# Layer-norm statistics of a convolution and mixture-of-experts kernel: from two matmul groups on TensorE to block transposes and free-axis sums on VectorE

## What is computed

```python
x = x + _L0_conv_ref(_ln_c(x), ...)
t = _to_tokens(x)
t = t + _L0_ffn_ref(_ln_t(t), ...)
...
def _ln_t(v, eps=1e-05):
    m = jnp.mean(v, axis=-1, keepdims=True)
    s = jnp.var(v, axis=-1, keepdims=True)
    return (v - m) / jnp.sqrt(s + eps)
```

## Time and profile before

| | us |
|---|---|
| median of 3 runs | 1285.11 (1285.0 to 1286.29) |
| profiled execution, its own time | 1287.97 |
| its span | 1286.2 |
| TensorE busy | 1251.1 (97%) |
| VectorE busy | 849.1 (66%) |
| ScalarE busy | 820.8 (64%) |
| GpSimd busy | 666.8 (52%) |

### The profile page before, as it was taken

One profiled execution on the slowest core, in us unless ns is written; L12 is line 12 of the kernel. 1 busy time (PEld: TensorE's weight loads), 2 busy tenths in 40 slices (PEclk: granted clock), 3 DMA queues, 4 the chain that ended last, 5 costly groups with the idle time before them and its releaser, 6 DMA issues. The chain is left out here.

```text
span 1286.2 us, 36567 instructions
## 1 busy us (share of the span) xinstructions
PE 1251.1 (97%) x14628; PEld 622.3 (48%) x14628; DVE 849.1 (66%) x1495; ACT 820.8 (64%) x1046; POOL 666.8 (52%) x607
## 2 busy tenths in 40 slices
PE   6999989999999999999999999999999999999897
PEld 4789744444444444444444444444444444444553
DVE  5444656676677677677677677677677777666554
ACT  5677756666666666666666666666667666666443
POOL 0151514645665655665655665655665655665532
PEclk9999999999999999999999999999999999999899
DMA  9897502332333332343342343332343333333211
GB/s 215 198 200 198 109 16 59 87 81 58 79 87 79 86 82 56 79 93 72 86 87 56 74 94 72 87 86 65 68 89 78 81 87 75 65 84 75 57 30 30
DMA packets 262694, 111.28 MB, mean 87 GB/s; under 512 B 243336, under 2 KB 247008, under 8 KB 262624
## 3 DMA queue, kind: packets, MB, share of 16 engines
q1 hardware_dynamic: 261360, 108.87, 37.8%
q0 software_dynamic: 1264, 1.61, 0.6%
HBM read 84.25 MB, written 26.17 MB: 86 GB/s over the span
## 5 line engine op out<-in xcount | busy, mean ns | idle before, releaser
L1031 DVE SCALAR_TENSOR_TENSOR v<-ps,negb,wb 128x448 f32<-128x448 f32 x896 | 573.2, 679 | 309.9 <-PE ps L642 307.3
L843 ACT ACTIVATE h<-ps,bias 128x896 f32<-128x896 f32 x448 | 450.2, 1005 | 292.5 <-PE ps L620 289.5
L660 PE MATMUL ps<-v,wo 64*64 64x448 f32 x3584 | 449.3, 541 | 7.1 <-issue 6.8
L620 PE MATMUL ps<-xn,w 64*64 64x448 f32 x3584 | 444.7, 542 | 2.2 <-issue 2.1
L642 PE MATMUL ps<-h,w 64*64 64x448 f32 x3584 | 444.4, 538 | 1.7 <-issue 1.3
L495 POOL TENSOR_TENSOR sums<-sums 128x448 f32<-128x448 f32 x112 | 127.9, 1142 | 306.2 <-ACT sums L849 306.2
L642 PEld LDWEIGHTS ps<-h,w 64*64 64x64 f32 x3584 | 170.7, 133 | 174.8 <-issue 156.1
L660 PEld LDWEIGHTS ps<-v,wo 64*64 64x64 f32 x3584 | 158.3, 133 | 173.5 <-issue 159.1
L620 PEld LDWEIGHTS ps<-xn,w 64*64 64x64 f32 x3584 | 141.7, 132 | 188.9 <-issue 187.4
L489 POOL TENSOR_TENSOR o<-xin,gconst 128x448 f32<-128x448 f32 x112 | 126.2, 1139 | 162.4 <-DMA out<-o 97.1
L499 POOL TENSOR_TENSOR o<-o,sums 128x448 f32<-128x448 f32 x112 | 133.6, 1193 | 8.8
(11 more groups left out here) (167 smaller groups left out, 552.1 us busy)
## 6 DMA issues: line engine op xcount, KB each, us to landing
xa<-in_x SPq DMA_DIRECT2D x128, 196.0 KB, 5.0
xin<-in_x SPq DMA_DIRECT2D x224, 112.0 KB, 2.8
out<-o SPq DMA_DIRECT2D x224, 112.0 KB, 2.5
spread<-rs_rows SPq DMA_DIRECT2D x108, 224.0 KB, 4.2
wb<-gate_rows SPq DMA_DIRECT2D x54, 112.0 KB, 2.8
rs_rows<-rs SPq DMA_DIRECT2D x54, 7.0 KB
gate_rows<-wT SPq DMA_DIRECT2D x54, 1.8 KB
rows<-in_L_ffn_g POOLq DMA_DIRECT2D x2, 256.0 KB, 4.7
```

Source lines behind the costliest of these rows:

```text
L620: last = mm(ps[64 * two:64 * two + 64, L1_BANKS + ab, 0:NG], w1[half, P * q + C * two:P * q + C * two + C], xn[half, s, g, :], start=True, ...
L660: last = mm(ps[64 * par:64 * par + 64, ACC_BANKS + low, 0:NG], wo[rows_, 2 * Q + d, :], v[rows_, u % 2, par, d, :], start=(Q == 0 and d == ...
L843: A(h[:, u % 2, i], ps[:, L1_BANKS:L1_BANKS + 2, 0:NG], ACT.Relu, bias=bias[:, 0, q:q + 1]).then_inc(h_done[i], 1)
L1031: last = V.scalar_tensor_tensor(out=v[:, u % 2, ab, d, :].rearrange("p (b w) -> p b w", w=W), in0=ps[:, L2_BANKS[ab] + d, 0:NG].rearrange( ...
```

## The change

From chunk 1 on the sums over the channels are no longer matmuls over the data. (Chunk 0, prepared ahead of the loop, keeps the old way.)

- Behind each x1, VectorE transposes the group in blocks of 32x32 into t (a block has 32 channels and 32 tokens), so that a partition holds a token of a block and the 32 channels lie along the free axis (`turned_done`). A reduce per group then adds them: 128x448 to 128x14, in token_sums (place **means**).
- ScalarE squares the transposed t instead of xin. GpSimd (`halve_powers`, behind `add_upper(k, 1)` and `add_upper(k, 2)`) adds one half of the 32 squares to the other, 128x448 out of two groups' 128x896, and VectorE reduces the rest (place **fold**), to 128x28 for two groups.
- TensorE adds only the two blocks of 32 channels of each row: two 64x64 matmuls by 112 columns at place 52, with same_token. They wait for `summed_done` and `powers_summed`.
- Variance, root and inverse are 128x56 instead of 128x448. VectorE turns the result (128x64) and SyncE writes it to rs_rows as 64 pieces of 128 bytes per half instead of 4 rows; the broadcast back has the same size.
- The places move: x1 from 16, 21, 36, 39 to 12, 18, 24, 30, that is ahead of the first taking of u2, u3, u4 and u5. inv from 58 and 60 to 60 alone. SyncE's order of loads and stores is as before, and so are t's places on ScalarE.

```diff
         LOOPED = (RP - 1 - 2) // 2 * 2
-        LOOP_SLOT = 128
+        LOOP_SLOT = 156
...
         STEADY = Schedule(
-            t=(9, 15, 21, 27), x1=(16, 21, 36, 39), power=(33, 43), sums=52,
-            var=54, root=56, inv=(58, 60), logits=85, gate=86, turn=89, wb=94)
+            t=(9, 15, 21, 27), x1=(12, 18, 24, 30), means=(36, 36, 42, 42), power=(33, 43), fold=(42, 48), sums=52,
+            var=54, root=56, inv=(60, 60), logits=85, gate=86, turn=89, wb=94)
...
+                def halve_powers(q, p):
+
+                    pool.wait_ge(squares_done, STEPS * q + p + 1)
+                    parts = spread[:, 2 * p:2 * p + 2].rearrange("p g (k two c) -> p two (g k) c", two=2, c=TOKENS // 2)
+                    nc.gpsimd.tensor_tensor(parts[:, 0], parts[:, 0], parts[:, 1], ALU.add).then_inc(powers_halved, 1)
...
                     add_upper(k, 1)
+                    if left > 1:
+                        halve_powers(k + 2, 0)
                     add_upper(k, 2)
+                    if left > 1:
+                        halve_powers(k + 2, 1)
...
                             pe.wait_ge(v_done[0], UNITS * (q - 1) + 2)
+                            pe.wait_ge(summed_done, G * (q - 1) + G)
+                            pe.sem_inc(sums_free, 1)
+                            pe.wait_ge(powers_summed, STEPS * (q - 1) + STEPS)
+                            pe.sem_inc(powers_free, 1)
+                            for hi in range(2):
+                                rows_ = slice(64 * hi, 64 * hi + 64)
+                                last = mm(ps[rows_, Y, 0:2 * G * BLOCKS], same_token[rows_].rearrange("p a c -> p (a c)"),
+                                          token_sums[rows_].rearrange("p a g k -> p (a g k)"), start=True, stop=True)
+                            last.then_inc(power_done, 1)
+                    if h == at.sums and at is AHEAD:
                         pe.wait_ge(x1_done, G * q + G + G)
...
                     for p in places_at(at.power, h):
-                        act.wait_ge(x1_done, G * q + 2 * p + 2 + G)
+                        act.wait_ge(turned_done, G * (q - 1) + 2 * p + 2)
                         act.wait_ge(u_done[p], q + 1)
...
+                        A(spread[:, 2 * p:2 * p + 2], t[:, 2 * p:2 * p + 2], ACT.Square, bias=-1.0).then_inc(squares_done, 1)
...
                                                op0=ALU.min, op1=ALU.add).then_inc(x1_done, 1)
+                        if at is STEADY:
+                            dve.wait_ge(x1_done, G * q + g + 1 + G)
+                            V.transpose(t[:, g], xg.rearrange("p b w -> p (b w)")).then_inc(turned_done, 1)
+                    for g in places_at(at.means, h):
+                        dve.wait_ge(turned_done, G * (q - 1) + g + 1)
+                        V.tensor_reduce(token_sums[:, 0, g, :], t[:, g].rearrange("p (k c) -> p k c", c=TOKENS), AX.X, ALU.add).then_inc(summed_done, 1)
+                    for p in places_at(at.fold, h):
+                        dve.wait_ge(powers_halved, STEPS * (q - 1) + p + 1)
+                        halved = spread[:, 2 * p:2 * p + 2].rearrange("p g (k two c) -> p two (g k) c", two=2, c=TOKENS // 2)[:, 0]
+                        V.tensor_reduce(token_sums[:, 1, 2 * p:2 * p + 2, :].rearrange("p g k -> p (g k)"), halved, AX.X, ALU.add).then_inc(powers_summed, 1)
...
+                            final.then_inc(turn_ready, 1)
+                            dve.wait_ge(turn_ready, q)
+                            V.transpose(rs_turned[:], token_rs[:]).then_inc(rs_done, 1)
```

More of the change, by code:

```diff
@@ L33 @@
 QUADS = E // 4
+TOKENS = 32
+BLOCKS = NG // TOKENS
 UNITS = G * QUADS
@@ L41, with __init__ @@
 class Schedule:
-    def __init__(self, t, x1, power, sums, var, root, inv, logits, gate, turn, wb):
-        self.t, self.x1, self.power, self.sums = t, x1, power, sums
+    def __init__(self, t, x1, means, power, fold, sums, var, root, inv, logits, gate, turn, wb):
+        self.t, self.x1, self.means, self.power, self.fold, self.sums = t, x1, means, power, fold, sums
         self.var, self.root, self.inv = var, root, inv
@@ L165, in metaformer_kernel @@
         squares_done = sem("squares_done")
+        turned_done = sem("turned_done")
+        summed_done = sem("summed_done")
+        powers_halved = sem("powers_halved")
+        powers_summed = sem("powers_summed")
+        powers_free = sem("powers_free")
+        turn_ready = sem("turn_ready")
+        zero_pad = sem("zero_pad")
         means_done = sem("means_done")
@@ L512, in chunk @@
                     add_upper(k, 1)
+                    if left > 1:
+                        halve_powers(k + 2, 0)
                     add_upper(k, 2)
+                    if left > 1:
+                        halve_powers(k + 2, 1)
                     if not left:
                         add_upper(k, G - 1)
+                for p in range(STEPS):
+                    halve_powers(1, p)
                 body_of_chunks(chunk)
@@ L867, in prep @@
                         A(t[:, g].rearrange("p (b w) -> p b w", w=W), yq, ACT.Relu, bias=OFFSET1, scale=SCALE).then_inc(t_done, 1)
-                    if h == at.sums:
+                    if h == at.sums and at is STEADY:
+                        act.wait_ge(power_done, q + 1)
+                        A(token_mean2[:], ps[:, Y, 0:G * BLOCKS], ACT.Square, bias=-1.0).then_inc(mean2_done, 1)
+                    if h == at.sums and at is AHEAD:
                         act.wait_ge(means_done, q + 1)
@@ L966, in _ @@
                 V.tensor_tensor(pick[:], row_of[0], row_of[1], ALU.add)
+                V.memset(token_rs[:], 0.0)
+                step(V.tensor_reduce(same_token[:, 0, :], ident[:].rearrange("p (j c) -> p c j", c=TOKENS), AX.X, ALU.add))
+                step(V.tensor_scalar(same_token[:, 0, :], same_token[:, 0, :], 1.0 / C, None, ALU.mult))
+                V.tensor_copy(same_token[:, 1, :], same_token[:, 0, :])
                 def image_stats(m, g):
@@ L1056, in prep @@
                     if h == at.inv[0]:
+                        var, half_, root = (vareps[:], sq[:], rs[:]) if at is AHEAD else (token_var[:], token_sq[:], token_rs[:, 0:G * BLOCKS])
                         dve.wait_ge(root_done, q + 1)
[L1059 to L1060 removed]
+                        V.tensor_tensor(half_, var, root, ALU.mult).then_inc(d_rs, 1)
                         dve.wait_ge(d_rs, RS_STEPS * q + 1)
[L1062 removed]
+                        V.scalar_tensor_tensor(out=half_, in0=half_, scalar=-0.5, in1=root, op0=ALU.mult, op1=ALU.mult).then_inc(d_rs, 1)
@@ L1063, in prep @@
                         dve.wait_ge(d_rs, RS_STEPS * q + 2)
-                        V.scalar_tensor_tensor(out=rs[:], in0=sq[:], scalar=1.5, in1=rs[:], op0=ALU.add, op1=ALU.mult).then_inc(rs_done, 1)
+                        final = V.scalar_tensor_tensor(out=root, in0=half_, scalar=1.5, in1=root, op0=ALU.add, op1=ALU.mult)
+                        if at is AHEAD:
+                            final.then_inc(rs_done, 1)
+                        else:
+                            final.then_inc(turn_ready, 1)
+                            dve.wait_ge(turn_ready, q)
+                            V.transpose(rs_turned[:], token_rs[:]).then_inc(rs_done, 1)
```

45 lines of the change are left out of this document (27 added, 18 removed).

## The result

The changed kernel takes 1325.46 us, the median of 4 runs (1321.01 to 1330.07), against 1285.7 us of the kernel before beside it (1285.0 to 1287.07). The ratio is 1.031, with a 95% interval of 1.027 to 1.035: slower by 40 us. The forecast was slower, 1312 us, with a range of 1288 to 1338. The profiled execution took 1330.07 us, the longest of the four and 4.6 us above their median, with a span of 1327.5 us. Against the profiled execution before (1286.2 us) the span grew by 41.3 us.

What follows compares the result with a forecast made beforehand. TensorE's order of steps was taken as the bound. Terms -43.2 (sums), +2.7 (variance wait), +65 (u4 load wait) and +2 (start) gave +26.5 on 1287.97, so 1314.5; less 2.86 for the median, 1312 us, range 1288 to 1338.

Steps and rivals of the forecast that it cites:

- Direction and cause: Slower: in u4, x1 of group 2 waits for its load, so TensorE waits in u5, chunks 0 to 25: +65 us.
- A second wait, of x1 of group 3: Group 3's load lands near 640.4, before VectorE asks for it at 641.7, so no second wait.
- Saving on TensorE: Sums cost 1.80 us a chunk, two new matmuls 0.2: 1.6 us saved in each of 27 chunks, -43.2 us.
- the wait for the variance: layer2 of u1 waits for VectorE's first variance instruction, some 0.1 us a chunk: +2.7 us over 27.
- Transpose and reduce: On VectorE, 0.62 us for each transpose and each reduce of 448 elements, ten of them a chunk, 6.2 us.
- The rival with a transpose of 1.09 us: 32x32 blocks of f32 pass VectorE at half speed, lengthening u4's wait and making u2 late: near 1330 us; chance 0.18.
- Places that fit: Added VectorE work in u2, u3, u5, u6, u7 and u0 stays inside the 2.65 us slack ahead of first takings.
- The size of TensorE's wait: With x1 at 1.17 us beside GpSimd in u4, TensorE waits 2.5 us a chunk in u5: +65 us.
- The clock: a rival with 0.05: Every wait in u5 drops TensorE to 1.2 GHz, 3 us more a chunk: 78 us, so 1390; chance 0.05.
- The start of the chunks: Ahead of chunk 0, three transposes, reduces and half-sums against shorter first sums: +2 us, between -2 and +6.
- the upper end, 1336: Transpose of 1.09, wait 3.0 us, u2 0.2 late, new matmuls at 0.45 so 36.5 saved: +51, or 1336.

Runs made afterwards that it cites:

- the places spread out: The changed kernel with x1=(12,18,30,42), means=(24,24,36,48), fold=(42,48), load queue unchanged: 1250.9 us against 1283.7 us before, ratio 0.974.
- the version with 2.4 us ahead of u7's takings: The changed kernel with x1 and transpose of group 2 in u6, of group 3 in u7, and reduces moved: 1267.5 us against 1287.1 us before, ratio 0.986.
- the version with the two loads earlier: The changed kernel with the load of group 2 ahead of store(k, 0) and group 3's right behind it: 1288.1 us against 1287.1 us before, ratio 1.002.
- the add in halves: The changed kernel with GpSimd's first add of feature (L492, 128x896) as two of 448 elements: 1311.9 us against 1287.1 us before, ratio 1.022.

## Why the prediction was right, and where it was off

- **Direction and cause: right.** The x1 of u4 that VectorE reaches before its load has landed, the place (ahead of u5's layer2, then its layer3), and the number of chunks (26) are in the trace as forecast: the idle time ahead of it was said to be about 3.4 us, and was 3.1 to 3.7 in all but one chunk. A second wait, of x1 of group 3, was ruled out, and came to at most 0.3 us where x1 of group 2 was short. Moving x1 alone in the kernel before shows that it costs time by itself, and with the places spread out the same work gives a gain.
- **Saving on TensorE: right.** From the layer2 ahead of the sums to that of u1 it was 4.11 us and is 2.55 (683.91 to 686.46 in the changed kernel, with 620.33 for the old end): 1.56 us a chunk, the wait for the variance included. The forecast had 1.6 less 0.1.
- **Transpose and reduce: right.** 0.62 us were taken for each, 0.645 and 0.604 measured, GpSimd's half-sum 1.145 for 1.14. The rival with a transpose of 1.09 us is out. For tensor_reduce the Trainium skill ("VectorE: DVE Perf Modes", Rules for kernel authors) advised restructuring; here 448 elements passed in 0.604 us, and what decided was whether they stood inside a unit's slack.
- **Places that fit: right for the units of the change**, except that the count left no room for waits on other engines: the version with 2.4 us ahead of u7's takings did wait 0.5 us there, under the 2.65. u5 kept to it, u7 did not.
- **The size of TensorE's wait: the step that failed.** The sum had 2.5 us in every chunk, 65 us in all, in which x1 at 1.17 us ("GpSimd is in L476 from 637.16 on") was taken as the price of an x1 beside GpSimd. There is no such price. x1 takes 0.6 us, or it stands still until the GpSimd instruction that is under way has ended and takes 0.49 us more. The earlier trace rows say it already: L499 ends at 632.23 and the x1 of 631.55 ends at 632.72. With L476's 2.09 us the upper bound was not 1.17 but 2.58. So TensorE loses some 2.0 us in the chunks with a short x1, which is less than forecast, and some 3.8 in those with a long one (38.8 and 40.6 us less 36.8), and which it is rests on a race of a few tenths between the landing and the start of L492. That the mean of the two, 2.7 us without the clock, is near the forecast's 2.5 is luck.
- **The clock: a rival with 0.05, in part true.** It fell in 10 of the 26 steady chunks at u5's wait: behind 2.63 and 3.08 us in chunks 0 and 1, behind 2.8 us or more in eight later ones, and never behind those of 1.1 to 1.7. At 1.5 us each that is some 15 us, not the 78 of "every chunk". It was priced as all or nothing, where the waits have two lengths. The Trainium skill ("TensorE: Matmul & The Clock Gate", HAM oscillation) tells of a DMA wait that sends the clock down in every turn of a loop; here it did so in some turns only.
- **The ends.** The start of the chunks moved by 193.43 - 191.56 = 1.9 us, for a forecast of 2. From the first chunk's sums to the last it is 1050.5 us for 1004.9, +45.6, and the stretch behind them is 6 us shorter. That the tail would gain was not foreseen.

The sum of it: the forecast of +26.5 us had the saving, the start and the cause, and put 65 us on waits that came to 86 (45.6 + 26 x 1.56). An estimate from the chunk times splits them into 2.0 us in each of 26 chunks (52), 1.8 in the 11 with the long x1 (20) and 1.5 in the 10 with the fallen clock (15). That 1325 us lies in the range is luck in part: the upper end, 1336, was made of a transpose of 1.09 us, which is out, and without it the bounds end near 1322 (the new matmuls at 0.45, and +6 ahead of chunk 0).

## What to carry to other kernels

When work is moved within a hand-written order, look for the latest arrival among its inputs before its own duration: the move that this change made for the sake of VectorE's load per unit put an instruction in front of its DMA, and everything behind it in the queue paid. Read off the slack at each place, and keep instructions that wait for a transfer behind it, not ahead of the work that the bounding engine wants next. A two-input VectorE instruction beside GpSimd is priced at up to the rest of GpSimd's longest instruction, not at a mean, and the short ones too: new work on GpSimd can make a 0.17 us instruction of VectorE last 1.12 us.

## What the runs showed of the hardware

- A VectorE instruction with two inputs in SBUF does not run slower beside GpSimd; it stands until GpSimd's has ended. In all 36 x1 of over 0.67 us in the changed kernel's trace, and all 71 in that of the kernel before, the end was 0.48 to 0.49 us behind the end of the GpSimd instruction that began before it, however long it had stood; for the gates' subtraction of 16 elements it was 0.03 us. When x1 began before L492, it was L492 that grew, from 2.08 to between 2.29 and 2.58 us. The transposes, with one input, took 644 to 647 ns in all 108 cases, 84 of them begun inside a GpSimd instruction. The Trainium skill ("SBUF — State Buffer", SBUF: two separate sides) states it as an exclusive lock that is held for the whole instruction, and the trace agrees; the forecast had not drawn on that page.
- The two DMAs of a group's load, 112 KB each, landed in 2.8 us in the median (2.7 to 3.9) directly behind a store in the kernel before, and in 4.2 us (3.3 to 4.7) directly behind four broadcasts of 224 KB in the version with the two loads earlier.
- In the changed kernel's trace the granted clock stayed at 2.4 GHz over the waits of TensorE of up to 1.7 us in u5, and fell to 1.2 GHz, for two to four steps, behind 8 of the 10 of 2.8 us or more in chunks 2 to 24 and behind those of 2.63 and 3.08 in chunks 0 and 1. The length of the wait does not decide alone: with the add in halves the clock fell behind 1.95 us in chunk 0 and stayed over 2.17 us in chunk 11. What decides between them no run here shows.
- Four runs of the changed kernel lay within 9 us of each other and four with the add in halves within 21, where 13 of the kernel before lay within 7. The race between the landing of a load and the start of a GpSimd instruction would do that, but since only one run of each kernel left a trace, it is not shown.
